# A decoder kernel's first layer: the interleaving tables of two streams, rewritten for four engines

## The chip, the cores and the metric

The kernel runs on one core of a Trainium2 chip. The time is the device time of one execution in microseconds (us). Profiles come from one profiled execution; its span runs from the first instruction's start to the last one's end, and the execution's own time is about 2 us longer than that.

## What is computed

The reference is a decoder of two layers over x of shape (8, 256, 256), eight batches of 256 tokens with 256 features, and a context of (8, 77, 192). Each layer is post-norm: after each block the input is added and a layer norm follows. Cut to what matters:

```python
def layer0(x, ctx):
    # mixer
    xz = x @ W_in.T                       # 256 -> 2 x 512
    xc, z = split(xz)
    xc = silu(causal_conv4(xc) + conv_b)
    B, C, dl = split(xc @ W_xproj.T)      # 16, 16, 512
    dl = softplus(dl)
    bc = sum(B * C, axis=-1)
    y = (dl * xc * bc + D * xc) * silu(z)
    x = layernorm(x + y @ W_out.T)
    # cross attention, 16 heads of 64, 77 context rows
    q, k, v = x @ Wq, ctx @ Wk, ctx @ Wv
    x = layernorm(x + softmax(q @ k.T / 8) @ v @ Wo + bo)
    # 8 experts, the best 2 of each token, and a shared one
    return layernorm(x + moe(x))
def layer1(x, ctx):
    # attention with rotary positions, cross attention, attention with a mask
    ...
```

Everything is float32. The change concerns the order in which the mixer and the cross attention of layer 0 are issued.

## The kernel before, in words

**Tiles and precision.** A batch is held as 2 x 128 tokens of 256 features in `xres` (float32). Matrix products take each operand as a rounded high half and a low half, so a product is three matmuls: high by high, high by low, low by high. ScalarE (ACT) rounds, at L1520; VectorE (DVE) forms the low half of data, at L1908; GpSimd (POOL) forms that of weights, at L2577 and L2633. TensorE (PE) has a few helpers: `mm3` (L169 to L171) issues the three matmuls together; `whole` (L175, L176) issues the two that need only the high half of the data, `rest` (L180) the third once the low half is there; L184, L185 and L189 are the same with the operands swapped; L193 to L197 project the context to keys and values, two batches and up to 308 columns wide. L869 is the transpose, L1064 the scores, L1080 the weighing of values.

**Steps.** Each engine has a generator per batch that issues one step and yields. I name a step by batch and name. In the mixer: xT (transpose of x, rounding, low half), xb (the half of W_in that feeds the convolution), z (the other half, in two steps), B, p0, p1 (the products with W_xproj; before B comes pB), g, sp, dl, yf (DVE's gating), y0, y1 (rounding), y (product with W_out), then add, bs/ba (statistics, L1933 and L1937), ve and rs (the power of the variance, POOL L2589 and L2592) and ln (scaling, DVE L1913). ACT's share of the mixer is also silu (L1560 and L1565), and abs, exp and ln of softplus (L1583, L1590, L1597). DVE's convolution stands at L1913 and L1916. In the cross attention, with X ahead: XxT, Xq0, Xq1 (query projection, two halves), Xs0 to Xs3 (scores of four heads each), Xm, Xu, Xn, Xr on DVE (maximum, subtraction, normalisation), p on POOL (L2616), Xt0 to Xt3 (transposes of the weights), Xo0 to Xo3 (weighing), Xy (product with Wo, one step for each of eight pieces), and POOL's bias add Xbias (L2582). The steps 0.k are the key projection of layer 0. K1.xy are the pieces of layer 1's context projections, made in between and evicted by DVE at L2008.

**Two streams.** Batches 0, 2, 4, 6 are the first stream and 1, 3, 5, 7 the second. Each has its own buffers; the program's names in the order lists below end in 0 and 1 for the two (`ps0`, `r10`, `m10` are the first stream's, `ps1`, `r11`, `m11` the second's). `x0_all(st)` runs `l0` (mixer) and `xattn` over the stream's four batches; the steps of one batch follow those of the batch before it. The streams are merged by `in_turn`:

```python
def in_turn(first, second, after):
    done = 0
    for want in after:
        while done < want:
            next(first, None)
            done += 1
        next(second, None)
```

The list `after` holds one number for each step of the second stream: so many steps of the first stream have been issued on this engine before that step. It is a fixed order, worked out ahead and written into the tables `FIRST` (L42, layer 0), `SECOND` and `LAST` (layer 1), each with a list for PE, ACT, DVE and POOL. `FIRST` is used at L1133 (PE), L1656 (ACT), L2129 (DVE) and L2644 (POOL). SyncE (SP) issues the loads in an order of its own; each waits on semaphores that steps raise. Each engine takes its instructions strictly in the order of the program, and waits between engines are semaphores that a step raises for its batch and name.

**The order before.** The lists of `FIRST` repeat from pair to pair: on PE the same pattern comes back with 59 added, on ACT with 46, on DVE with 63, on POOL with 17. So the pairs 2/3, 4/5 and 6/7 are issued alike, and the pair 0/1 differs where weights still have to come in.

Of the kernel before, what the change touches and what calls it, by code (L numbers as in the profile page):

```python
# [40 lines left out]

FIRST = {  # L42
# [7 lines left out]
    "ACT": [  # L50
# [5 lines left out]
    "DVE": [  # L56
# [7 lines left out]
    "POOL": [  # L64
        1, 4, 5, 8, 9, 11, 13, 13, 13, 13, 13, 13, 15, 16, 16, 16, 16, 18, 21, 22, 25, 26, 28, 30, 30, 30, 30, 30, 30, 32, 33, 33, 33, 33, 35, 38, 39, 42, 43, 45,
        47, 47, 47, 47, 47, 47, 49, 50, 50, 50, 50, 52, 55, 56, 59, 60, 62, 64, 64, 64, 64, 64, 64, 66, 67, 67, 67, 67],
}
SECOND = {
# [2797 lines left out]
```

How the kernel before makes its waits and increments, by code:

```python
        def last_x0(eng):  # L658
            for st in streams:
                eng.wait_ge(*st.x_dve[0].at(st.batches[-1], "ln"))
# [1 line left out]
        def last_moe(eng):  # L662
            eng.wait_ge(*r_pe.at("dn", NT - 1))
            for st in streams:
                eng.wait_ge(*st.n_dve.at(st.batches[0], "ln"))
            eng.wait_ge(*w1s["lo"].at("wp"))
# [1 line left out]
        def last_x1(eng):  # L668
            for st in streams:
                eng.wait_ge(*st.x_pe[1].at(st.batches[-1], "y"))
# [1 line left out]
        def last_q(eng):  # L672
            for st in streams:
                eng.wait_ge(*st.q_dve.at(st.batches[-1], "sim"))
                eng.wait_ge(*st.q_act.at(st.batches[-1], "c2"))
                eng.wait_ge(*st.q_pool.at(st.batches[-1], "bias"))
                eng.wait_ge(d_kp[st.i], 16 * 4)
# [3 lines left out]
        @block.sync  # L681
# [14 lines left out]
            def store0(what, u):  # L696
                slot, done, _ = slot0(what, u)
                sp.wait_ge(*(kv_evk.at(what, u, 3) if what == "k" else kv_ev[0].at(what, u, 1)))
                if what == "k":
                    store_keys(0, u, slot, done)
                else:
                    sp.dma_start(vd[0, P * u:P * (u + 1), :], slot[:, 0:1024]).then_inc(done, 16)
# [1 line left out]
            def store1(u):  # L704
                slot, done, _ = slot1(u)
                sp.wait_ge(*kv_ev[1 if u < 6 else 2].at(u, 3 if u < 4 else 2))
                if u < 4:
                    store_keys(1, u, slot, done)
                else:
# [80 lines left out]
            sp.wait_ge(*gate_dve.at("idx"))
```

## Time and profile before

| | before |
|---|---|
| median of 3 executions (lowest to highest) | 1506.3 us (1503.81 to 1506.79) |
| the profiled execution's own time | 1508.33 us |
| its span | 1506.3 us |
| mean granted TensorE clock, share of full speed | 0.925 |
| PE busy | 1325.1 us (88% of the span) |
| PE weight loads busy | 1098.4 us (73%) |
| DVE busy | 972.1 us (65%) |
| ACT busy | 649.8 us (43%) |
| POOL busy | 424.8 us (28%) |
| chain of work that ended last | PE 69%, DVE 19%, ACT 6% |
| instructions | 27793 |

Busy time is that of one engine's instructions over the whole span; PE's weight loads lie beside its matmuls. The chain of work that ended last is followed back from the last instruction to what released it, so its shares say what the end waited for. Layer 0's mixer and cross attention, which the changed tables order, take about the first 430 us of the span; the rest is layer 0's experts and layer 1. The granted clock has two levels, 1.2 and 2.4 GHz; a share of 0.50 in a stretch is the lower one throughout.

### The profile page before, as it was taken

How to read it: one execution, taken by the hardware profiler on the slowest of the kernel's cores; microseconds unless marked ns; L12 is line 12 of the kernel's file. 1: busy time of each engine (PE TensorE's matmuls, PEld its weight loads, DVE VectorE, ACT ScalarE, POOL GpSimd, SP SyncE). 2: the span in 40 equal slices, each digit the busy share in tenths (PEclk: the TensorE clock that was granted, in tenths of full speed). 3: DMA queues.
4: the chain of work that ended last, by engine and by line, in shares of the span. 5: the costliest groups of instructions: out<-in, count | busy, mean ns of one | idle time of the engine just before them, and what ended most of it. 6: DMA issues, size and time to landing. Idle time of an engine off the chain costs nothing.

```text
span 1506.3 us, 27793 instructions
## 1 busy us (share of the span) xinstructions
PE 1325.1 (88%) x11854; PEld 1098.4 (73%) x11854; DVE 972.1 (65%) x1785; ACT 649.8 (43%) x806; POOL 424.8 (28%) x405
## 2 busy tenths in 40 slices
PE   6899999998989999998789889879978958878886
PEld 6788889888878889997478658748847844646563
DVE  3776767867675446776765946757575645567573
ACT  6554556455542435662244145234334432341513
POOL 5141030310323744675023512703511330000000
PEclk9989999999999999998799899989989965887868
DMA  9371210111060315883001200200200120010000
GB/s 293 134 237 35 48 35 18 32 34 51 1 230 29 109 46 194 276 263 95 11 1 39 67 1 18 81 7 1 77 1 1 43 85 27 18 57 16 2 16 15
DMA packets 46138, 103.33 MB, mean 69 GB/s; under 512 B 4336, under 2 KB 26480, under 8 KB 45120
## 3 DMA queue, kind: packets, MB, share of 16 engines
q1 hardware_dynamic: 42944, 93.18, 18.8%
q0 software_dynamic: 3072, 8.39, 1.7%
q8 instruction: 93, 1.52, 0.4%
q14 instruction: 29, 0.24, 0.0%
HBM read 64.79 MB, written 36.77 MB: 67 GB/s over the span
## 4 chain that ended last, share of the span: by engine, by line
PE 69%; DVE 19%; ACT 6%; POOL 2%; issue 2%; DMA 1%; SPq 0%; POOLq 0%; DVEq 0%; ACTq 0%
DVE sm L1919 9%; PE ps L869 9%; PE ps L169 8%; PE ps L170 8%; PE ps L171 8%; PE ps L1336 4%; PE ps L1064 4%; PE ps L1080 4%; PE ps L184 4%; PE ps L1342 4%; PE ps L189 4%; PE ps L185 3%; ACT m L1778 2%; DVE m L1908 2%; PE ps L175 2%
## 5 line engine op out<-in xcount | busy, mean ns | idle before, releaser
L1520 ACT ACTIVATE m<-ps 128x1024 f32<-128x1024 f32 (+4 forms) x208 | 165.6, 812 | 306.5 <-PE ps L171 107.2
L1919 DVE TENSOR_REDUCE sm<-ps 128x8 f32<-128x2048 f32 (+1 forms) x128 | 193.5, 1533 | 45.3 <-PE ps L1317 25.2
L2589 POOL TENSOR_SCALAR sm<-sm 128x2 f32<-128x2 f32 x40 | 8.8, 219 | 687.0 <-DVE sm L1937 687.0
L1908 DVE TENSOR_TENSOR r<-ps,r 128x512 fp32r<-128x512 f32 (+1 forms) x159 | 116.3, 739 | 122.5 <-ACT r L1520 122.4
L1520 ACT ACTIVATE r<-ps 128x512 fp32r<-128x512 f32 (+1 forms) x159 | 100.9, 639 | 208.1 <-PE ps L869 104.8
L1778 ACT ACTIVATE m<-ps 128x2048 f32<-128x2048 f32 x64 | 119.2, 1876 | 143.2 <-PE ps L1336 143.0
L869 PE MATMUL ps<-cst,m 128*77 128x128 f32 (+2 forms) x1024 | 136.4, 276 | 14.9 <-DVE m L2357 3.6
L869 PEld LDWEIGHTS ps<-cst,m 128*77 128x77 f32 (+2 forms) x1024 | 114.2, 146 | 39.0 <-issue 15.0
L1317 PE MATMUL ps<-m 32*128 32x256 f32 x1024 | 106.3, 553 | 33.3 <-DVE sm L1919 28.7
L1317 PEld LDWEIGHTS ps<-m 32*128 32x128 f32 x1024 | 65.4, 261 | 69.6 <-DVE sm L1919 54.4
L2616 POOL TENSOR_TENSOR m<-m,sm 128x616 f32<-128x616 f32 x64 | 77.0, 1216 | 126.3 <-DVE sm L2092 126.0
L1336 PE MATMUL ps<-m 32*128 32x256 f32 x1024 | 85.8, 465 | 26.1 <-DVE m L2357 22.8
L2357 DVE COPY m<-ps 128x256 f32<-128x256 f32 x64 | 26.9, 422 | 116.9 <-PE ps L1342 116.9
L1336 PEld LDWEIGHTS ps<-m 32*128 32x128 f32 x1024 | 56.2, 221 | 54.8 <-DVE m L2357 42.4
L1342 PE MATMUL ps<-m 128*32 128x256 f32 x1024 | 72.7, 404 | 11.5 <-ACT m L1778 11.1
L1908 DVE TENSOR_TENSOR xres<-ps,xres 128x256 f32<-128x256 f32 (+1 forms) x112 | 51.4, 494 | 48.2 <-PE ps L189 45.5
L169 PE MATMUL ps<-r,w0h 128*128 128x256 f32 x288 | 81.3, 282 | 0.0
L170 PE MATMUL ps<-r,w0h 128*128 128x256 f32 x288 | 81.3, 282 | 0.0
L171 PE MATMUL ps<-r,w0l 128*128 128x256 f32 x288 | 81.1, 282 | 0.0
L169 PE MATMUL ps<-xTall,uw 128*128 128x512 f32 (+1 forms) x216 | 76.1, 352 | 0.2 <-DVE xres L1908 0.2
L170 PE MATMUL ps<-xTall,uw 128*128 128x512 f32 (+1 forms) x216 | 74.9, 347 | 0.0
L171 PE MATMUL ps<-xTall,uw 128*128 128x512 f32 (+1 forms) x216 | 74.7, 346 | 0.0
(322 smaller groups left out, 3606.9 us busy)
## 6 DMA issues: line engine op xcount, KB each, us to landing
raw<-wu_dram SPq DMA_DIRECT2D x20, 768.0 KB, 5.7
keep_dram<-m SPq DMA_DIRECT2D x8, 768.0 KB, 3.7
m<-keep_dram SPq DMA_DIRECT2D x8, 768.0 KB, 4.3
xs_dram<-gsq SPq DMA_DIRECT2D x2, 2944.0 KB, 18.3
ys_dram<-m SPq DMA_DIRECT2D x23, 256.0 KB, 3.1
room<-wu_dram SPq DMA_DIRECT2D x7, 768.0 KB, 4.7
rt<-xs_dram SPq DMA_DIRECT2D x16, 256.0 KB, 3.4
w1raw<-w_dram SPq DMA_DIRECT2D x1, 3840.0 KB, 11.7
```

Source lines behind the costliest of these rows:

```text
L169: pe.matmul(o, l[0], r[0], start=start, stop=False)
L170: pe.matmul(o, l[0], r[1], start=False, stop=False)
L171: return pe.matmul(o, l[1], r[0], start=False, stop=stop)
L869: return pe.transpose(o, i, ident[0:n, 0:n])
L1317: m = pe.matmul(bank(st, a)[:, 256 * j:256 * j + 256], v.qT[r:r + 32, c, 128 * j:128 * j + 128], v.kT[r:r + 32, c, :], start=True, stop=True)
L1336: m = pe.matmul(bank(st, a)[:, 256 * k:256 * k + 256], v.kT[r:r + 32, c, 128 * k:128 * k + 128], v.qT[r:r + 32, c, :], start=True, stop=True)
L1342: m = pe.matmul(bank(st, c)[32 * a:32 * a + 32, 0:256], v.va[:, k, 4 * c + a, :], w[:, a, k, :], start=k == 0, stop=k == 1)
L1520: return act.activation(o, i, ACT.Copy)
L1778: act.activation(v.P, st.ps[:, :], ACT.Exp, scale=0.25).then_inc(sig.up(b, f"e{c}"), 1)
L1908: return dve.tensor_tensor(o, a, b_, op)
L1919: return dve.tensor_reduce(o, i, AX.X, op, **kw)
L2616: pool.tensor_tensor(pw, pw, v.rc[u].unsqueeze(2).to_broadcast([P, 8, CK]), ALU.mult).then_inc(sig.up(b, f"p{u}"), 1)
```

## The change

The four lists of `FIRST` are replaced. No step, instruction, buffer or wait is added or taken away; only where the second stream's steps stand among the first's. The new lists do not repeat from pair to pair: each engine's covers all four batches of a stream. The start of the diff, which says little by itself:

```diff
 FIRST = {
     "PE": [
-        6, 6, 6, 6, 6, 6, 19, 19, 19, 19, 21, 21, 21, 21, 23, 23, 23, 27, 28, 29, 32, 32, 32, 32, 32, 37, 41, 41, 41, 42, 42, 42, 43, 43, 43, 44, 48, 51, 53, 53,
+        5, 6, 6, 6, 6, 6, 21, 21, 21, 21, 21, 21, 21, 21, 23, 23, 23, 27, 27, 27, 27, 27, 27, 27, 38, 38, 40, 40, 40, 40, 41, 41, 41, 41, 43, 47, 47, 49, 53, 53,
...
```

**At the start, on PE.** Behind the key projection of layer 0 (the matmuls of 308 columns) and the transpose of batch 1 (`ps1<-cst,xres`), and ahead of batch 1's product with W_in. One piece of the difference; the twelve added rows are the second half of 0.z, four times these three:

```order
 L197 MATMUL ps1<-ctxB,w0l 128x308
 L869 MATMUL ps1<-cst,xres 128x128 x4
+L169 MATMUL ps0<-r10,w0h 128x256
+L170 MATMUL ps0<-r10,w0h 128x256
+L171 MATMUL ps0<-r10,w0l 128x256
...
 L175 MATMUL ps1<-r11,w0h 128x256
 L176 MATMUL ps1<-r11,w0l 128x256
```

The same twelve are gone from ahead of the key projection, where both halves of 0.z stood before.

**At the first norm, on PE.** From batch 0's product with W_out (0.y) to what follows it. Before:

```order
L184 MATMUL ps0<-w0h,r10 128x256
L185 MATMUL ps0<-w0l,r10 128x256
...
L189 MATMUL ps0<-w0h,r10 128x256 x8
L869 MATMUL ps0<-cst,xres 128x128 x4
L175 MATMUL ps0<-r10,w0h 128x256
L176 MATMUL ps0<-r10,w0l 128x256
```

And of the change:

```order
L189 MATMUL ps0<-w0h,r10 128x256 x8
L184 MATMUL ps1<-w0h,r11 128x256
L185 MATMUL ps1<-w0l,r11 128x256
...
L189 MATMUL ps1<-w0h,r11 128x256 x8
L869 MATMUL ps0<-cst,xres 128x128 x4
```

Batch 1's product with W_out (1.y, 24 matmuls, `ps1`) now stands between 0.y and the transpose 0.XxT; before it stood behind 0.Xq0.

**The same place on DVE.** `m11` and `r11` are batch 1's gating and its low half, the `xres<-ps0,xres` rows batch 0's add, `BN_STATS` and `BN_AGGR` its statistics. Before:

```order
L2000 COPY stage<-ps1 128x512
L1908 TENSOR_TENSOR xres<-ps0,xres 128x256 x2
L1933 BN_STATS sm0<-xres 128x6 x2
L1937 BN_AGGR sm0<-sm0 128x2 x2
L1916 SCALAR_TENSOR_TENSOR m11<-ps1,m11 128x512 x2
L1913 TENSOR_SCALAR xres<-xres,sm0 128x256 x2
L1908 TENSOR_TENSOR m11<-m11,ps1 128x512 x2
L1908 TENSOR_TENSOR r10<-ps0,r10 128x512
L1916 SCALAR_TENSOR_TENSOR m11<-m11,w0f 128x256 x4
L1908 TENSOR_TENSOR r11<-m11,r11 128x512 x2
L1908 TENSOR_TENSOR xres<-ps1,xres 128x256 x2
```

And of the change:

```order
L2000 COPY stage<-ps1 128x512
L1916 SCALAR_TENSOR_TENSOR m11<-ps1,m11 128x512 x2
L1908 TENSOR_TENSOR m11<-m11,ps1 128x512 x2
L1916 SCALAR_TENSOR_TENSOR m11<-m11,w0f 128x256 x2
L1908 TENSOR_TENSOR xres<-ps0,xres 128x256
L1916 SCALAR_TENSOR_TENSOR m11<-m11,w0f 128x256 x2
L1908 TENSOR_TENSOR xres<-ps0,xres 128x256
L1933 BN_STATS sm0<-xres 128x6 x2
L1937 BN_AGGR sm0<-sm0 128x2 x2
L1908 TENSOR_TENSOR r11<-m11,r11 128x512 x2
L1913 TENSOR_SCALAR xres<-xres,sm0 128x256 x2
L1908 TENSOR_TENSOR xres<-ps1,xres 128x256 x2
```

Batch 1's gating and low halves stand ahead of batch 0's scaling now; before, most of them stood behind it.

**In a later pair, on ACT.** Batches 2 and 3, at the rounding of batch 3's transpose (3.xT, `r11<-ps1`). Before:

```order
L1520 ACTIVATE m10<-ps0 128x4x256
L1560 ACT_TABLE_LOAD
L1560 ACTIVATE m10<-ps0 128x1024
L1520 ACTIVATE r11<-ps1 128x512
L1565 ACTIVATE m10<-m10 128x512
L1520 ACTIVATE r10<-m10 128x512
```

And of the change:

```order
L1520 ACTIVATE m10<-ps0 128x4x256
L1520 ACTIVATE r11<-ps1 128x512
L1560 ACT_TABLE_LOAD
L1560 ACTIVATE m10<-ps0 128x1024
L1565 ACTIVATE m10<-m10 128x512
L1520 ACTIVATE r10<-m10 128x512
```

The rounding of 3.xT stands ahead of silu of batch 2's z now; before it stood behind it. On PE, 3.xT stands between the two halves of 2.z; before, behind both.

Further on in each pair, 3.y stands behind 2.Xq1 on PE, 3.g on DVE moves ahead of the first eviction of K1, and in the pairs 4/5 and 6/7 POOL's bias add stands ahead of the powers of the norm. In the attention stretches neighbouring rows of the two streams are swapped on PE, ACT and DVE. The order of SP is the same as before.

## Rows read from the trace of the kernel before

**Rows 1.** Busy us of each engine by stretch (the first line names columns).

```profile
core 0: us, PE busy (x) PEld busy (x) DVE busy (x) ACT busy (x) POOL busy (x), PEclk, DMA share, GB/s
95.00:133.00 38.00, 37.90 (x306) 32.30 (x306) 24.37 (x46) 19.18 (x26) 15.15 (x15) 1.00 0.27 89
133.00:190.00 57.00, 52.12 (x407) 49.17 (x406) 46.57 (x105) 33.04 (x47) 4.55 (x9) 1.00 0.15 32
323.00:380.00 57.00, 51.42 (x411) 48.88 (x410) 46.50 (x103) 33.13 (x47) 4.57 (x9) 1.00 0.11 34
```

**Rows 2.** PE's instructions in order of time, 17 to 95 us: start, duration, instruction, wait before.

```profile
17.33 0.28 PE L169 MATMUL ps<-r,w0h 128*128 128x256 f32 x1
...
18.62 0.28 PE L171 MATMUL ps<-r,w0l 128*128 128x256 f32 x1
19.85 0.38 PE L193 MATMUL ps<-ctxAh,w0h 128*128 128x308 f32 x1 [0.95 <-POOL w0l L2633]
...
32.16 0.30 PE L197 MATMUL ps<-ctxB,w0l 128*128 128x308 f32 x1
...
34.33 0.39 PE L175 MATMUL ps<-r,w0h 128*128 128x256 f32 x1 [0.69 <-ACT r L1520]
...
76.90 1.12 PE L869 MATMUL ps<-cst,xres 128*128 128x128 f32 x4 [6.04 <-DVE xres L1913]
78.77 0.58 PE L175 MATMUL ps<-r,w0h 128*128 128x256 f32 x1 [0.75 <-ACT r L1520]
...
83.66 0.28 PE L184 MATMUL ps<-w0h,r 128*128 128x256 f32 x1
...
94.85 0.39 PE L175 MATMUL ps<-r,w0h 128*128 128x256 f32 x1
```

**Rows 3.** The same view, the pair of batches 2 and 3.

```profile
140.75 0.39 PE L175 MATMUL ps<-r,w0h 128*128 128x256 f32 x1 [1.16 <-ACT r L1520]
...
155.93 0.41 PE L193 MATMUL ps<-ctxAh,kw1h 128*128 128x308 f32 x1 [0.64 <-DVE stage L2008]
...
171.66 0.41 PE L193 MATMUL ps<-ctxAh,kw2h 128*128 128x308 f32 x1 [1.17 <-DVE stage L2008]
...
173.50 0.66 PE L869 MATMUL ps<-cst,xres 128*128 128x128 f32 x4 [0.87 <-DVE xres L1913]
...
174.91 0.39 PE L175 MATMUL ps<-r,w0h 128*128 128x256 f32 x1
...
178.03 0.36 PE L184 MATMUL ps<-w0h,r 128*128 128x256 f32 x1
```

**Rows 4.** ACT, POOL and DVE in order of time, ahead of row 76.90.

```profile
68.59 1.90 ACT L1520 ACTIVATE w0h<-w0raw 128x2048 fp32r<-128x2048 f32 x1
...
70.57 4.51 POOL L2577 TENSOR_TENSOR w0l<-w0raw,w0h 128x2048 fp32r<-128x2048 f32 x1 [29.11 <-ACT w0h L1520]
...
76.11 0.74 DVE L1913 TENSOR_SCALAR xres<-xres,sm 128x256 f32<-128x256 f32 x2 [2.61 <-POOL sm L2592]
```

**Rows 5.** Stretches as in rows 1 (PEclk third from last), and PE's waits.

```profile
70.00:74.00 4.00, 0.87 (x8) 0.66 (x6) 2.99 (x8) 0.49 (x1) 3.43 (x1) 0.87 1.01 342
74.00:82.00 8.00, 4.35 (x19) 3.95 (x20) 5.09 (x11) 1.86 (x3) 2.00 (x3) 0.50 1.03 288
82.00:84.00 2.00, 2.00 (x14) 2.00 (x14) 0.40 (x1) 0.14 (x1) 0.00 (x0) 0.71 1.08 386
430.00:434.00 4.00, 3.73 (x17) 1.47 (x18) 4.00 (x5) 3.25 (x4) 3.01 (x1) 1.00 0.87 265
690.00:692.00 2.00, 0.60 (x3) 0.60 (x3) 1.34 (x3) 0.60 (x1) 0.00 (x0) 0.69 0.00 0
...
430.27 0.40 PE L169 MATMUL ps<-xTall,rwr 128*8 128x512 f32 x1 [1.54 <-DVE xTall L1908]
691.40 0.58 PE L169 MATMUL ps<-xTall,r 128*128 128x256 f32 x1 [3.48 <-DVE r L1908]
```

**Rows 6.** DVE's scaling and POOL's bias add, batches 2 and 1.

```profile
183.62 1.46 POOL L2582 TENSOR_TENSOR xres<-xres,w0f 128x256 f32<-128x256 f32 x2
...
183.68 1.55 DVE L1913 TENSOR_SCALAR xres<-xres,sm 128x256 f32<-128x256 f32 x2 [1.14 <-POOL sm L2592]
```

More of the change, by code:

```diff
@@ L43 @@
     "PE": [
[6 rows of a table removed]
-    "ACT": [
[5 rows of a table removed]
-    "DVE": [
[7 rows of a table removed]
[6 rows of a table added]
+    "ACT": [
[5 rows of a table added]
+    "DVE": [
[7 rows of a table added]
     "POOL": [
-        1, 4, 5, 8, 9, 11, 13, 13, 13, 13, 13, 13, 15, 16, 16, 16, 16, 18, 21, 22, 25, 26, 28, 30, 30, 30, 30, 30, 30, 32, 33, 33, 33, 33, 35, 38, 39, 42, 43, 45,
-        47, 47, 47, 47, 47, 47, 49, 50, 50, 50, 50, 52, 55, 56, 59, 60, 62, 64, 64, 64, 64, 64, 64, 66, 67, 67, 67, 67],
+        3, 3, 3, 12, 12, 12, 12, 12, 12, 12, 12, 12, 15, 15, 15, 20, 20, 20, 20, 20, 26, 26, 26, 26, 29, 29, 29, 29, 29, 32, 32, 32, 41, 41, 41, 41, 41, 46, 46, 46,
+        46, 46, 46, 46, 46, 46, 49, 49, 49, 54, 54, 54, 54, 54, 58, 58, 58, 58, 63, 63, 63, 63, 63, 66, 66, 66],
 }
```

34 rows, old and new, of the table FIRST are left out of this document.

## The prediction, made before the changed kernel was run

> **What bounds the kernel now.** I began with the busy shares by stretch for the first layer, the only part that the change touches [rows 1]. In the stretch that holds a pair's four-head attention (95 to 133 us) TensorE (PE) is busy for 37.90 of 38 us, and later ones look alike: there is nothing to win there, only something to lose. In the stretches that hold a pair's mixer, its projections and the first scores (133 to 190 us, the pair of batches 2 and 3, and 323 to 380 us, that of 6 and 7) it is busy for 52.12 and 51.42 of 57 us, with VectorE (DVE) at about 46.5 beside it. The reader should see that PE's slack in the steady part is about 5 us in each of three pairs, some 15 us in all, and that DVE, at 82% and in strict order, often sets when PE goes on.
>
> Next came PE's rows in order of time, for the waits in brackets. At the start three matter [rows 2]: 0.95 us for the key weights' low half, which GpSimd (POOL) finishes at 19.71; 6.04 us before the transpose of batch 0 for its cross attention; 0.75 us behind that. In the pair of batches 2 and 3 the four longest are 1.16, 0.64, 1.17 and 0.87 us [rows 3]. I call a step by its batch and name, as in the lists of the kernel.
>
> The 6.04 us end in a chain that no order can shorten [rows 4]: ScalarE (ACT) rounds wq at 68.59, POOL forms its low half in 4.51 us, then takes the power for batch 0's norm, DVE scales, and PE may start at 76.90. While PE waits, its clock falls. The mean granted clock is 0.87 from 70 to 74 us, 0.50 from 74 to 82 and 0.71 from 82 to 84 [rows 5], that is, 1.2 GHz from 73.0 to 83.2 us.
>
> **The change, part by part.** Matmuls of 256 columns start 0.118 us apart at 2.4 GHz: the twelve of the second half of 0.z from 17.33 to 18.62 [rows 2]. So the 24 of batch 1's output projection are 24 x 0.118 = 2.8 us. The 24 of 0.Xq0 started at 78.77, and the next step at 83.66 [rows 2], 0.20 us for each, almost all at 1.2 GHz.
>
> *The second half of 0.z moves behind the key projection.* It is 12 matmuls, 1.41 us. Before, they ran between 17.3 and 18.9, while PE would have waited for POOL's low half anyway (row 19.85 is released by it). Now that wait grows from 0.95 to about 2.4 us, and the 12 run after 1.xT, around 33.6. There a wait of 0.69 us for ACT's rounding covers half of them, so PE goes on 0.75 us later. PE stays without a longer wait up to 1.p1, whose result ACT needs before the exponentials, wq and so the chain of [rows 4]: **+0.75 us**. ACT's silu of batch 0 also moves behind wout's rounding, which puts 0.ln1 off by about 1.7 us; DVE takes it some 2 us after it was ready before, so I cost this at nothing. Its cover is thin, and without it the excess over 2 us is added one for one.
>
> *The longer wait may drop the clock.* Bounds come from the trace. After a wait of 1.54 us the clock stayed at 2.4 GHz (1.00 from 430 to 434); in the wait of 6.04 us it fell 2.1 us after the last matmul; in one of 3.48 us it fell after 2.9 us, and was 0.69 over 690 to 692 [rows 5]. The new wait of 2.4 us lies between. If the clock stays, the cost is 0. If it falls at about 21 us, the key projection, which PE did from 19.85 to about 32.5 without a wait [rows 2], runs at roughly 0.55 of their pace; a low stretch of 6.8 us then costs 3.1 us, one of 10.2 us (as that of [rows 5]) 4.6 us. I take 1.2 us, a little under half of the first, since 2.4 us is about midway between the wait that kept the clock and the one that lost it: **+1.2 us**, ends 0 and 4.6. The Trainium skill, page "TensorE: Matmul & The Clock Gate", part 1, says that the array is throttled by default, that sustained activity releases it and idleness takes that back; it speaks against making this wait longer. Read so that the new wait counts as idleness, the term would be 3.1 and the sum -1.35 instead of -3.25 us.
>
> *Batch 1's output projection moves into the 6.04 us.* Before, 0.y was followed by 0.XxT and 0.Xq0, and only then by 1.y. Now 1.y comes first, and DVE takes 1.sp, 1.dl and 1.yf ahead of batch 0's norm. Step by step, without the two terms above: ACT has 1.y0 at about 73.1 and 1.y1 at 74.3, behind wq. DVE has its part of both by 76.4, because batch 0's adds and statistics stand between; POOL's power is ready at about 76.3, and 0.ln ends at 77.1, 0.3 later than before. PE's last eight matmuls of 1.y end at about 77.6. So 0.XxT starts 0.7 us later than 76.90, and the 2.8 us behind it are gone: -2.1. The clock decides the rest: 0.XxT and 0.Xq0 took 1.12 and 4.9 us at 1.2 GHz [rows 2], against 0.66 and 3.1 for batch 2 at the high one [rows 3]. If 1.y's matmuls, spread over the gap, keep the clock up, another 2.3 us go (-4.4); if not, 1.y itself runs slowly and the gain stays at about -2.0. I take the middle, **-3.2 us**, for want of a row nearer to either.
>
> *The order inside each later pair.* The transpose 3.xT now stands between the halves of 2.z, 1.41 us earlier, and ACT rounds it ahead of silu: the wait of 1.16 us [rows 3] goes. What is late next is DVE, which finishes the convolution of batch 2 no sooner. PE then waits about 0.6 us for DVE's 2.xr1, about 0.6 for the first key eviction, now behind the new place of 3.g, and 0.7 each for K1.10 and 2.ln. It reaches the scores 2.Xs0 some 1.7 us earlier. But 3.y now runs after 2.Xq1, so 3.ln falls among the maxima of batch 2. With POOL's bias add beside it that scaling takes 1.55 us [rows 6] instead of the 0.74 of [rows 4], and PE waits about 1 us for 2.Xu0 and 1 us for 3.ln. What is left at 3.Xq0 is about -0.4 us for this pair. For batches 4 and 5 POOL does the bias add ahead of the norm, which takes it out of that collision, so I take -0.9; for 6 and 7, -0.7. Sum **-2.0 us**. Bounds: nothing but the 15 us of waits can be won, and at most a third of them in a chain that DVE paces at 82%, -5; and if the waits at the scores come out 1 us longer in each pair, +1.
>
> *The attention stretches.* All rows that PE, ACT and DVE swap there have PE work to cover them (37.90 of 38 us busy); cost nothing. In the worst place, 0.Xr2 now stands behind 1.Xm0 on DVE, and so POOL's p3 comes some 3 us later, just as PE needs it. Without this cover each us is lost one for one. POOL's and SP's queues carry the same work; SP's order is unchanged, and every load it issues hangs on a semaphore of these steps, so the rest of the program follows the shift.
>
> **Sum.** +0.75 +1.2 -3.2 -2.0 = -3.25 us. The profiled execution took 1508.33 us, its span 1506.3 and 2.0 around it, so it would be 1505.1. It stands 2.0 above the median of the runs shown (1506.3); I carry the difference over: 1506.3 - 3.25 = **1503.0 us**.
>
> **The rivals.**
> - *The gap is filled at the high clock and nothing falls before it.* For: 1.y spreads its 24 matmuls over the gap, and the first wait is barely longer than 2 us. Against: the clock fell 2.1 us into a wait once. Terms: +0.75 +0 -4.4 -2.0 = -5.65: 1500.7.
> - *DVE paces the pairs, and only the start gains.* For: DVE's share of 82%, and that my walk gave back 1.3 of 1.7 us within ten rows. Against: the first wait of each pair plainly goes. Terms: +0.75 +1.2 -3.2 +0 = -1.25: 1505.1.
> - *Slower: the clock falls on the key projection.* One mechanism, at 19 to 32 us on PE: the wait grown to 2.4 us drops the clock for a stretch like that of [rows 5], 4.6 us are lost where PE alone sets the end, and the later gap is filled with slow matmuls. Terms: +0.75 +4.6 -2.0 +0 = +3.35: 1509.7. It decides from the point where more than about 2 us of the first wait are enough to lose the clock and the low stretch lasts over about 6 us. The Trainium skill's page named above would allow it; rows for a wait of just this length are wanting.
>
> **How the numbers follow.** Forecast 0.52, first rival 0.20, second 0.18, third 0.10. A measurement can tell about 0.2%, 3.0 us. The forecast lies right at that bound: its own range is 1501.5 to 1504.5, and I give it 0.30 to faster and 0.22 to the same. Faster 0.30 + 0.20 = 0.50, same 0.22 + 0.18 = 0.40, slower 0.10. The range that should hold 8 in 10 runs from the first rival, with a little more from the pairs (their end of -5 taken half), to just beyond the second: 1499.5 to 1506.5.
>
> **What would show it.** Right: PE's wait before 0.XxT splits into pieces of at most 2.5 us with 1.y between, 1.Xq0 starts 2 to 4.5 us earlier than 94.85, and the wait of 1.16 us before 3.xb is gone. The granted clock from 18 to 32 us says which rival holds: 1.00 throughout speaks for the first, 0.50 over half of it for the third. In the pairs, PE idle in 57 us should go from 4.9 to 4.0 to 4.5 us. Wrong: first keys starting later than 19.85, a wait of over 2 us at 1.pB or 0.Xt0, or PE idle over 1 us in an attention stretch.

## The result and the profile after

The changed kernel took 1493.27 us in the median of five executions (1490.48 to 1496.0), the kernel before 1503.81 (1502.96 to 1506.79) beside it: ratio 0.9919, with a 95% interval of 0.9903 to 0.9935, or 12 us (10 to 15) of 1504. A second series with the unaltered changed kernel gave 0.9927 (0.9902 to 0.9952). I had predicted 1503.0 us, in a range of 1499.5 to 1506.5. It is faster, as forecast, but by 10 to 15 us and not by 3, and lies outside the range.

The page of the changed kernel, its busy times:

```profile
span 1491.3 us, 27793 instructions
PE 1307.7 (88%) x11854; PEld 1088.9 (73%) x11854; DVE 972.4 (65%) x1785; ACT 651.8 (44%) x806; POOL 426.5 (29%) x405
```

The spans of the two profiles differ by 15.0 us. To find where, I took the end of every step from PE's rows in order of time, in both traces. The last step of layer 0's cross attention (7.Xy) ends at 421.07 before and at 411.60 after: 9.5 us. The remaining 5.5 us arise in code that the change does not touch, most of them behind 1360 us; the kernel with only the start changed, below, shows 5.1 of them too. What lies behind 7.Xy took 1085.2 us in the profile of before and 1078.6 to 1085.2 us in the other thirteen profiles of this document. So the 5.5 us are within what one execution differs from the next, with a lower clock beside them (0.77 before against 0.85 after from 1250 to 1400 us), and no part of the explanation. So the question is where 9.5 us come from. By stretch:

| PE's stretch, us | before | changed | gain | predicted |
|---|---|---|---|---|
| start of the keys to end of 1.bc | 45.68 | 46.93 | -1.25 | -1.95 |
| end of 1.bc to end of 1.Xy | 68.01 | 65.84 | +2.17 | +3.2 |
| pair 2/3 (1.Xy to 3.Xy) | 94.64 | 93.01 | +1.63 | +0.4 |
| pair 4/5 | 94.63 | 91.32 | +3.31 | +0.9 |
| pair 6/7 | 98.26 | 94.63 | +3.63 | +0.7 |

The start did about what was said of it in the sum, though not term by term. The pairs gave 8.6 us where I had 2.0. The busy shares, changed kernel (the first row answers to the second of [rows 1], the last to its third; 228 to 285 us was 52.12 of 57 before):

```profile
133.00:190.00 57.00, 53.42 (x417) 50.35 (x417) 47.96 (x109) 33.00 (x47) 6.17 (x10) 1.00 0.15 33
228.00:285.00 57.00, 54.94 (x433) 52.31 (x433) 48.85 (x109) 35.88 (x51) 6.18 (x9) 1.00 0.12 33
323.00:380.00 57.00, 54.69 (x436) 51.77 (x435) 48.95 (x103) 36.39 (x52) 9.51 (x12) 1.00 0.11 34
```

PE's slack, the first number against the second, went from 4.9, 4.9 and 5.6 us to 3.6, 2.1 and 2.3. DVE is busier (48.9 of 57 us), since the same work now fits in less time. PE's rows in order of time with a wait of over 0.25 us, changed kernel, pairs 2/3, 4/5 and 6/7, against [rows 3]:

```profile
145.99 0.44 PE L180 MATMUL ps<-r,w0h 128*48 128x256 f32 x2 [0.28 <-DVE r L1908]
...
163.64 0.36 PE L184 MATMUL ps<-w0h,r 128*128 128x256 f32 x1 [0.87 <-DVE stage L2008]
...
168.90 0.41 PE L193 MATMUL ps<-ctxAh,kw2h 128*128 128x308 f32 x1 [0.64 <-DVE stage L2008]
...
170.12 0.66 PE L869 MATMUL ps<-cst,xres 128*128 128x128 f32 x4 [0.26 <-DVE xres L1913]
...
183.80 1.31 PE L1064 MATMUL ps<-m 128*128 128x154 f32 x8 [0.75 <-DVE m L1908]
...
185.81 0.66 PE L869 MATMUL ps<-cst,xres 128*128 128x128 f32 x4 [0.69 <-DVE xres L1913]
...
260.82 0.41 PE L193 MATMUL ps<-ctxAh,kw2h 128*128 128x308 f32 x1 [0.64 <-DVE stage L2008]
...
262.36 0.41 PE L193 MATMUL ps<-ctxAh,kw2h 128*128 128x308 f32 x1 [0.57 <-DVE stage L2008]
...
264.20 0.41 PE L193 MATMUL ps<-ctxAh,kw2h 128*128 128x308 f32 x1 [0.42 <-DVE m L1916]
...
268.40 0.36 PE L184 MATMUL ps<-w0h,r 128*128 128x256 f32 x1 [0.26 <-issue]
...
353.13 0.39 PE L193 MATMUL ps<-kw2h,ctxAh 128*128 128x256 f32 x1 [0.85 <-DVE stage L2008]
...
355.37 0.39 PE L193 MATMUL ps<-kw2h,ctxAh 128*128 128x256 f32 x1 [0.35 <-DVE stage L2008]
...
368.81 1.31 PE L1064 MATMUL ps<-m 128*128 128x154 f32 x8 [0.88 <-DVE m L1908]
```

The wait of 1.16 us before 3.xb is gone in all three pairs. In 2/3 the two waits at the scores are there that the prediction named (183.80 for 2.Xs2, 185.81 for 3.XxT); in 4/5 neither is.

At the start, PE's rows and two stretches (as in [rows 5]):

```profile
19.87 0.38 PE L193 MATMUL ps<-ctxAh,w0h 128*128 128x308 f32 x1 [3.41 <-POOL w0l L2633]
...
77.33 0.55 PE L184 MATMUL ps<-w0h,r 128*128 128x256 f32 x1 [5.20 <-ACT r L1520]
...
82.26 0.60 PE L869 MATMUL ps<-cst,xres 128*128 128x128 f32 x4
83.60 0.38 PE L175 MATMUL ps<-r,w0h 128*128 128x256 f32 x1 [0.75 <-ACT r L1520]
```

```profile
20.00:22.00 2.00, 2.00 (x10) 2.00 (x11) 2.00 (x6) 1.51 (x2) 0.00 (x0) 0.59 1.04 440
22.00:24.00 2.00, 2.00 (x10) 2.00 (x9) 2.00 (x7) 0.77 (x2) 0.70 (x1) 0.55 0.82 278
```

The wait for the keys' low half is 3.41 us and not 2.4 (x landed 0.7 us earlier in this execution, so PE had finished sooner), and the clock fell behind it, to 0.59 and 0.55 over four microseconds. 1.y does stand in the gap now, but starts only at 77.33, behind a wait of 5.20 us.

### The profile page after: what moved, and what is told of

It reads as the page before. It is cut to its first block, busy times and chain, and to the rows that moved or that the text cites. A ratio compares the mean times of both kernels' runs of the same rounds, so it can differ in the third digit from the quotient of the medians.

```text
span 1491.3 us, 27793 instructions
## 1 busy us (share of the span) xinstructions
PE 1307.7 (88%) x11854; PEld 1088.9 (73%) x11854; DVE 972.4 (65%) x1785; ACT 651.8 (44%) x806; POOL 426.5 (29%) x405
## 3 DMA queue, kind: packets, MB, share of 16 engines
q8 instruction: 93, 1.52, 0.4%
## 4 chain that ended last, share of the span: by engine, by line
PE 32%; DVE 15%; ACT 3%; POOL 2%; issue 1%; DMA 0%; POOLq 0%; DVEq 0%; SPq 0%; ACTq 0%
DVE sm L1919 9%; PE ps L869 6%; PE ps L1336 4%; PE ps L1342 4%; ACT m L1778 2%; PE ps L184 2%; PE ps L1064 2%; PE ps L189 2%; PE ps L1080 2%; PE ps L185 2%; DVE m L1908 2%; PE ps L1455 1%; PE ps L1317 1%; DVE m L2357 1%; PE ps L171 1%
## 5 line engine op out<-in xcount | busy, mean ns | idle before, releaser
L1317 PE MATMUL ps<-m 32*128 32x256 f32 x1024 | 102.5, 536 | 34.7 <-DVE sm L1919 30.2
L1317 PEld LDWEIGHTS ps<-m 32*128 32x128 f32 x1024 | 64.2, 256 | 68.8 <-DVE sm L1919 54.5
L1336 PE MATMUL ps<-m 32*128 32x256 f32 x1024 | 82.6, 449 | 27.5 <-DVE m L2357 23.5
L1336 PEld LDWEIGHTS ps<-m 32*128 32x128 f32 x1024 | 53.5, 210 | 55.7 <-DVE m L2357 43.2
```

What stands on the lines that cost most here:

```text
L1317: m = pe.matmul(bank(st, a)[:, 256 * j:256 * j + 256], v.qT[r:r + 32, c, 128 * j:128 * j + 128], v.kT[r:r + 32, c, :], start=True, stop=True)
L1336: m = pe.matmul(bank(st, a)[:, 256 * k:256 * k + 256], v.kT[r:r + 32, c, 128 * k:128 * k + 128], v.qT[r:r + 32, c, :], start=True, stop=True)
```

## The experiments

Steps' ends, stretches and waits below are read from each run's own trace; they repeat to 0.1 us in the pairs. Edits are given in short form: `new` and `old` are the tables of the changed kernel and of before, and a list is cut where the first step of batch 3 stands (PE 60, ACT 45, DVE 62 or 63, POOL 17 or 18 entries).

### The start alone, and the pairs alone

```diff
-FIRST = new
+FIRST = {e: new[e][:cut[e]] + old[e][cut[e]:] for e in new}
```

> The new order for batches 0 and 1, the order of before for the pairs 2/3, 4/5 and 6/7. My theory, from the two traces laid beside each other: the start gains only about 0.9 us by 133 us, since 1.26 us lost behind the key projection stand against some 2 us won at the first norm. So the time should be 0.5 to 1.5 us below before, ratio 0.999 to 1.000, and the pair 2/3 should show its 4.8 us of PE idle again. Rival: the start sets the stage for the pairs (a different phase between the engines), and more than 3 us of the gain comes with it: ratio below 0.998.

Ratio 0.9997 (0.9984 to 1.0009). 1.Xy ends 2.7 us earlier than before, and the pairs 2/3 and 4/5 last as before, 94.62 and 94.61 us. (6/7 took 99.81, 1.6 more: three waits of 0.91, 0.99 and 0.75 us in a row stand there as before, but in this execution the clock fell behind them, 0.89 from 355 to 370 us.) The rival falls.

```diff
-FIRST = new
+FIRST = {e: old[e][:cut[e]] + new[e][cut[e]:] for e in new}
```

> The order of before for batches 0 and 1, the new order for the three later pairs. My theory: the pairs carry the gain, 1.3 us in the pair 2/3, 3.3 in 4/5 and 3.6 in 6/7, together about 8.2 us by 430 us, where I had predicted 2.0: ratio about 0.994 to 0.995. Rival, that the gain hangs on the start: less than 4 us, ratio above 0.997.

Ratio 0.9947 (0.9935 to 0.9959), 8.0 us (6 to 10). The pairs last 93.01, 91.32 and 94.65 us, to 0.02 us those of the changed kernel. In the traces the two parts are independent, and the pairs carry the gain. The times do not quite add up: 0.5 us (-1.4 to 2.4) and 8.0 us make 8.5, where the whole change gave 12 (10 to 15). The traces have the start alone at 2.7 us, more than its time shows; the rest of the difference stays open.

### The second half of 0.z back

```diff
 "PE": [
-    5, 6, 6, 6, 6, 6, 21, 21, ...
+    6, 6, 6, 6, 6, 6, 21, 21, ...
```

> The changed kernel with one number of PE's list put back, so that both halves of 0.z run ahead of the key projection again; ACT still takes silu of batch 0 behind the rounding of wout. My theory: the 3.41 us of PE idle ahead of the first keys shrink to about 2, the clock stays at 2.4 GHz over 20 to 24 us (1.00 instead of 0.50), and 1.xb starts 0.9 to 1.5 us earlier: 1 to 2 us faster than the changed kernel. Rival: the wait of about 2 us still loses the clock, and then only the 0.45 us of the moved half come back. Second rival: ACT's evictions pace the keys in any case (the wait of 0.78 us before), and nothing is won at 1.xT.

Ratio 0.9916 (0.9904 to 0.9929), no difference that the times can tell from the changed kernel, so the 1 to 2 us that I expected are not in them. The trace tells more. From the start of the keys to that of 1.xT PE took 13.13 us before, 13.60 in the changed kernel's profile, and 12.10 here, 12.05 with the start alone. So with the clock held, the new start is 1.1 us faster than before in this stretch: ACT's silu of batch 0 now stands behind the evictions, and this wait for an eviction, in the trace of before, is gone:

```profile
23.71 0.41 PE L193 MATMUL ps<-ctxAh,w0h 128*128 128x308 f32 x1 [0.78 <-ACT stage L1520]
```

No run moved silu alone, so that it is the cause is read from the rows and not tested. By the end of 1.bc the 1.1 us can no longer be seen: from the start of the keys it is 44.88 to 45.74 us in seven profiles with the changed start and the clock kept, and 45.67, 45.16 and 45.22 in the three with the old start. The fall of the clock costs 1.5 us on top. The half of 0.z costs 0.4 us at the end of 1.xb (16.55 us from the start of the keys here, 16.97 with the start alone), and at 1.bc nothing of it is left: 45.06 against 45.18.

The clock over the keys hangs on the wait ahead of them. PE's row of the first key, and the stretch of 20 to 24 us behind it, for the start alone:

```profile
19.81 0.38 PE L193 MATMUL ps<-ctxAh,w0h 128*128 128x308 f32 x1 [2.44 <-POOL w0l L2633]
```

```profile
20.00:24.00 4.00, 4.00 (x30) 4.00 (x30) 4.00 (x12) 3.01 (x6) 0.76 (x1) 1.00 0.94 362
```

and for the run with POOL's old order, whose start is that of the changed kernel:

```profile
19.20 0.38 PE L193 MATMUL ps<-ctxAh,w0h 128*128 128x308 f32 x1 [2.53 <-POOL w0l L2633]
```

```profile
20.00:24.00 4.00, 4.00 (x20) 4.00 (x19) 4.00 (x11) 1.97 (x5) 1.36 (x1) 0.57 0.90 343
```

2.53 and 3.41 us lost the clock; 2.44, 2.25, 1.82, 1.66, 1.40 and less kept it, in the other runs. Each is one execution, and nothing lies between.

### The norm ahead of the gating

```diff
 "DVE": [
-    2, 2, 7, 9, 9, 9, 9, 9, 10, 13, 14, 21, 21, 21, 21, 21, 21, 21, 22, 26, ...
+    2, 2, 7, 9, 9, 9, 9, 9, 10, 13, 14, 21, 21, 21, 21, 21, 21, 26, 26, 26, ...
```

> The changed kernel with two numbers of DVE's list raised: batch 0's adds, statistics and their aggregation stand ahead of 1.yf0 and 1.yf1. In the changed kernel one instruction of 1.yf0, a scalar_tensor_tensor with both operands in SBUF, took 3.80 us instead of 0.47, and ended at 76.13, just behind POOL's low half of wq (to 75.85). My theory: such an instruction stands still while POOL's runs, and one with an operand in PSUM, or with a single operand, does not. Then here the adds and statistics take their usual 0.41 and 0.43 us beside POOL, 1.yf0 ends at about 76.2 as before, 0.ln ends some 2.5 us earlier, at about 79, and 0.XxT starts 2 to 3 us earlier than 82.25: 2 to 3 us faster than the changed kernel. Rival: the long instruction waited for something else (its operand, a DMA), the adds are held up just as it was, and nothing is won.

What this run was for, first in the changed kernel: DVE in order of time, POOL in order of time, and all DVE instructions of line 1916 with operands in SBUF (shortest, median and longest in ns).

```profile
71.14 1.28 DVE L1908 TENSOR_TENSOR m<-m,ps 128x512 f32<-128x512 f32 x2
72.33 4.20 DVE L1916 SCALAR_TENSOR_TENSOR m<-m,w0f 128x256 f32<-128x256 f32 x2
76.45 0.41 DVE L1908 TENSOR_TENSOR xres<-ps,xres 128x256 f32<-128x256 f32 x1
...
78.02 0.75 DVE L1933 BATCH_NORM_STATS2 sm<-xres 128x6 f32<-128x256 f32 x2
```

```profile
71.34 4.51 POOL L2577 TENSOR_TENSOR w0l<-w0raw,w0h 128x2048 fp32r<-128x2048 f32 x1 [28.92 <-ACT w0h L1520]
```

```profile
L1916 DVE SCALAR_TENSOR_TENSOR m<-m,w0f x128: 466/477/3801, 20.1 to 359.4; 128x256 f32<-128x256 f32 x128
```

And with the norm first, DVE, POOL and PE:

```profile
70.53 0.75 DVE L1908 TENSOR_TENSOR xres<-ps,xres 128x256 f32<-128x256 f32 x2
71.31 0.75 DVE L1933 BATCH_NORM_STATS2 sm<-xres 128x6 f32<-128x256 f32 x2
...
72.20 3.32 DVE L1916 SCALAR_TENSOR_TENSOR m<-m,w0f 128x256 f32<-128x256 f32 x4
```

```profile
69.53 4.51 POOL L2577 TENSOR_TENSOR w0l<-w0raw,w0h 128x2048 fp32r<-128x2048 f32 x1 [28.70 <-ACT w0h L1520]
```

```profile
75.53 0.55 PE L184 MATMUL ps<-w0h,r 128*128 128x256 f32 x1 [5.20 <-ACT r L1520]
...
79.08 1.63 PE L189 MATMUL ps<-w0h,r 128*128 128x256 f32 x8
...
80.55 0.60 PE L869 MATMUL ps<-cst,xres 128*128 128x128 f32 x4
```

The first half of the theory holds. Adds (from PSUM) and statistics (one operand) run at their usual length beside POOL's 4.51 us, while the gating, both of whose tensors are in SBUF, stands still until POOL ends (69.53 + 4.51 = 74.04). The Trainium skill, page "SBUF — State Buffer", section "SBUF: two separate sides", says that DVE and GpSimd share one pair of ports, which an instruction of DVE with two inputs in SBUF, or GpSimd's own, holds for its whole length while the other waits. The rows agree, POOL's start of 71.34 and DVE's end of 76.13 (72.33 + 3.80) among them.

The second half falls. Ratio 0.9912 (0.9899 to 0.9925), the same as the changed kernel's, and from the end of 1.bc to that of 1.Xy PE took 66.00 us against 65.84. The statistics were ready early, but PE still had 1.y ahead of 0.XxT, from 75.53 to 80.55, the clock at 0.50 from 74 to 80 us. What sets this place, by these rows, is the chain wq's low half, gating, rounding, 1.y.

### POOL's low half of wq in eight pieces

```diff
-pool.tensor_tensor(lo[:, a:a + n], raw[:, a:a + n], hi[:, a:a + n], ALU.subtract)
+k = n // 8 if name == "wq" else n
+for a in range(a, a + n, k):
+    pool.tensor_tensor(lo[:, a:a + k], raw[:, a:a + k], hi[:, a:a + k], ALU.subtract)
```

> The changed kernel, where POOL forms the low half of wq in eight instructions of 256 columns instead of one of 2048 (4.51 us). The run with the norm first showed the adds at their usual 0.41 us beside POOL, 1.yf0 standing still until POOL's end, and nothing won, because PE's 1.y, at 1.2 GHz, sets when 0.XxT may start. My theory: DVE's instructions with both operands in SBUF get in between two of POOL's, so none takes over about 1.1 us; 1.yf0 ends some 2 us earlier, and so do 1.y and 0.XxT: 1.5 to 2.5 us faster than the changed kernel, whose clock may even stay up. Rival: POOL keeps its place from one instruction to the next, 1.yf0 still ends with the last of the eight, and nothing is won or 0.5 us lost to the shorter instructions.

DVE, POOL and PE:

```profile
69.90 1.56 DVE L1916 SCALAR_TENSOR_TENSOR m<-m,w0f 128x256 f32<-128x256 f32 x2
```

```profile
68.90 6.81 POOL L2579 TENSOR_TENSOR w0l<-w0raw,w0h 128x256 fp32r<-128x256 f32 x8 [29.15 <-ACT w0h L1520]
```

```profile
72.28 0.36 PE L184 MATMUL ps<-w0h,r 128*128 128x256 f32 x1 [2.57 <-ACT r L1520]
```

Now the two engines take turns: the gating pair takes 1.56 us instead of 4.20, POOL 6.81 for its eight, and PE's wait is 2.57 instead of 5.20. Yet 1.bc to 1.Xy took 66.14 us, no less than 65.84. The clock fell at about 73.2 all the same (0.80 from 72 to 74 us) and stayed at 1.2 GHz to about 83.4 (0.50 from 74 to 80, 0.57 from 80 to 84), with hardly a wait in between; the work starts earlier and runs slowly for longer. Ratio 0.9902 (0.9882 to 0.9922), which the times cannot tell from 0.9919. So in this execution taking the port's share away won nothing.

It can win something, as the last run below shows, which has the eight instructions too. There PE's wait before 1.y is 2.57 us again, and in both 0.XxT starts 13.60 us behind the end of 1.bc, against 14.95 to 15.79 in the nine profiles with one instruction and 1.y ahead of 0.XxT. But there the clock, low from about 72.7 us, was back at about 76.1. The same stretch of this run and of the last one:

```profile
76.00:84.00 8.00, 7.25 (x34) 6.37 (x33) 3.97 (x12) 0.60 (x1) 2.00 (x4) 0.54 1.07 350
```

```profile
76.00:84.00 8.00, 6.60 (x53) 6.13 (x53) 3.70 (x11) 1.62 (x2) 1.72 (x4) 0.99 1.07 360
```

From 1.bc to 1.Xy the last run took 64.04 us, less than any of those nine (65.32 to 66.59). So the port holds 1.y up by 2.6 us and 0.XxT by 1.4 to 2.2, and when the clock comes back decides whether this is still there at the end. Each is one execution, and the times resolve neither.

### One engine's order at a time

```diff
-FIRST = new
+FIRST = {e: old[e] for e in new}
+FIRST["PE"] = old["PE"][:60] + new["PE"][60:]
```

> The kernel before with one list changed: PE takes the new order in the pairs 2/3, 4/5 and 6/7; ACT, DVE and POOL keep theirs. My theory: the order of PE and that of DVE and ACT gain together, because the steps that PE now takes early (3.xT, 2.pB, 2.y, 2.XxT) have to be made ready early by the others. Alone it should give less than 3 of the 8.6 us, and may cost: 3.xT is still rounded behind silu, so the wait before 3.xb stays. Rival: the gain is PE's order alone (work of the other stream put into its waits), and then this kernel comes within 2 us of the one with the new pairs alone, ratio about 0.995.

Ratio 1.0155 (1.0136 to 1.0175), 23 us slower. The pairs last 105.35, 101.25 and 103.81 us. PE's rows, pair 2/3:

```profile
140.97 0.38 PE L175 MATMUL ps<-r,w0h 128*128 128x256 f32 x1 [1.60 <-ACT r L1520]
...
175.84 1.12 PE L869 MATMUL ps<-cst,xres 128*128 128x128 f32 x4 [2.91 <-DVE xres L1913]
...
193.60 2.42 PE L1064 MATMUL ps<-m 128*128 128x154 f32 x8 [3.64 <-DVE m L1908]
```

PE asks for 3.xT, the norm and the scores in the new order while ACT and DVE still make them in the old one. In this pair it is idle for 11.7 us instead of 5.0, and busy for 93.7 us instead of 89.7 with the same instructions: behind the last two of these waits the clock was low (the rows take 1.12 and 2.42 us instead of 0.66 and 1.31). The rival falls far.

```diff
-FIRST["ACT"] = new["ACT"]
+FIRST["ACT"] = new["ACT"][:45] + old["ACT"][45:]
```

> The changed kernel with ACT's old order in the three later pairs. In the prediction, ACT's rounding of 3.xT ahead of silu was what took away the wait of 1.16 us. My theory: that wait comes back in each pair (about 1.1 us before 3.xb, 5.xb, 7.xb), and with it half of it or more at the end of each pair: 2 to 4 us slower than the changed kernel, ratio 0.994 to 0.995 against before. Rival: what follows waits for DVE anyway and the 1.1 us are absorbed, so under 1 us in all.

Ratio 1.0045 (1.003 to 1.0061): the whole gain is gone and more. The pairs last 98.36, 100.06 and 102.60 us, 5.4, 8.7 and 8.0 more than in the changed kernel. The wait at 3.xb came back, longer (1.60 us), but so did others: 1.25 and 1.68 us for DVE's evictions, 1.24 us for ACT's rounding before 3.Xy. I had the direction and a small part of the size. ACT, busy 43% of the time, decides as much as PE's own order.

```diff
-FIRST["POOL"] = new["POOL"]
+FIRST["POOL"] = new["POOL"][:18] + old["POOL"][18:]
```

> The changed kernel with POOL's old order in the three later pairs: the bias adds of 4 and 6 stand behind the powers of 5's and 7's norm again. In the prediction this move was worth 0.5 us for 4/5 and 0.3 for 6/7. My theory now: it is worth little, 0 to 1 us in all, since PE in 4/5 has no wait at 5.XxT. Rival: it is the reason why 4/5 gains 3.3 us and 2/3 only 1.6; then PE's waits at 4.Xs2 and 5.XxT come back (0.7 us each, as at 2.Xs2 and 3.XxT) and the kernel is 2 to 3 us slower than the changed one.

Ratio 0.9914 (0.9896 to 0.9932), as the changed kernel. Only 4/5 is longer, by 0.45 us (91.77), with a wait of 0.37 us at 5.XxT. The rival falls; the size in the prediction, 0.5, was right for 4/5, and the 0.3 for 6/7 is nothing (94.61). The old order of PE alone, or of DVE alone, among the new ones was not tried.

### The order of 4/5 for 2/3 too (three_45)

```diff
+shift = {"PE": 59, "ACT": 46, "DVE": 63, "POOL": 17}
-FIRST[e] = new[e]
+FIRST[e] = new[e][:cut[e]] + [w - shift[e] for w in pair45[e]] + pair45[e] + pair67[e]
```

> The changed kernel, where the pair 2/3 takes the order that the changed kernel has for 4/5, on all four engines. In the changed kernel 2/3 gained 1.6 us and 4/5 3.3. My theory: up to the first scores both gain alike, about 2 us; 2/3 then gives 0.7 back, because PE waits for 2.Xs2 (0.75) and 3.XxT (0.69) while DVE still has 3's norm beside the first maxima, and in 4/5 the whole of 5.XxT and 5.Xq0 stands ahead of 4.Xs2 and covers it. Then 2/3 should gain 3.0 to 3.5 us here, both waits should be gone, and the kernel be 1.4 to 1.9 us faster than the changed one, ratio about 0.991. Rival: the pair 2/3 is another case (batch 1's attention ahead of it ends otherwise, SP's loads are later), the order is out of step with it, and it gains no more than 1.6.

Pair 2/3, PE's waits of over 0.25 us, the whole list:

```profile
166.15 0.41 PE L193 MATMUL ps<-ctxAh,kw2h 128*128 128x308 f32 x1 [0.64 <-DVE stage L2008]
...
167.69 0.41 PE L193 MATMUL ps<-ctxAh,kw2h 128*128 128x308 f32 x1 [0.57 <-DVE stage L2008]
...
169.53 0.41 PE L193 MATMUL ps<-ctxAh,kw2h 128*128 128x308 f32 x1 [0.43 <-DVE m L1916]
...
173.72 0.36 PE L184 MATMUL ps<-w0h,r 128*128 128x256 f32 x1 [0.27 <-issue]
```

The pair lasts 91.29 us, 3.35 less than before and the same as 4/5, and the waits at 2.Xs2 and 3.XxT are gone. The theory holds in the trace to 0.1 us. The time, 0.9924 (0.9903 to 0.9945), does not resolve 1.7 us.

### The old order in the first half of each pair

```diff
-FIRST[e] = new[e]
+FIRST[e] = new[e] with, in each later pair, the old entries up to PE 22, ACT 17, DVE 30
```

> The changed kernel with the old order in the first half of each later pair (PE, ACT and DVE up to the second y and the second ln; POOL and the attention new). My theory: about 1.7 of the 3.3 us of a pair come from the mixer half (3.xT between the halves of 2.z, with ACT's rounding ahead of silu, and y earlier), the rest from the half with the scores. So each pair should show the wait of 1.16 us again and gain 1 to 2 us less than in the changed kernel: 3 to 5 us slower than that. Rival: the halves do not fit together (as with PE's new order alone) and the kernel is slower than before.

Ratio 1.0016 (0.9999 to 1.0033). The wait of 1.16 us is back in each pair. 4/5 lasts 93.08 us, a gain of 1.55 for the half with the scores alone, as the theory says. But 2/3 lasts 98.24 and 6/7 99.13 us, 3.6 and 0.9 longer than before; in 2/3 PE waits 3.65 us at 2.Xs2. DVE's rows say why. Batch 3's add comes first, then batch 2's first maximum; the third row is the add of batch 5:

```profile
181.49 0.90 DVE L1908 TENSOR_TENSOR xres<-ps,xres 128x256 f32<-128x256 f32 x2 [4.32 <-PE ps L189]
...
185.99 0.78 DVE L1919 TENSOR_REDUCE sm<-ps 128x8 f32<-128x616 f32 x1
...
277.01 0.89 DVE L1908 TENSOR_TENSOR xres<-ps,xres 128x256 f32<-128x256 f32 x2 [1.52 <-PE ps L189]
```

In 2/3 this mixed order ends 3.y on PE behind 2.Xq1, while DVE still takes all of batch 3's norm ahead of batch 2's maxima: DVE waits 4.32 us for PE, and then PE 3.65 us for DVE. In 4/5 all of 5.y stands ahead of 4.Xq1, and DVE waits 1.52 us. In 6/7 PE's waits are those of before (5.5 against 5.6 us of those over 0.25), so the half with the scores wins nothing there; the 0.9 us are the clock, 0.72 from 364 to 370 us in this execution. So the split into halves is borne out in one pair only, and in 2/3, where the halves were not made for one another, the rival is right.

### The changed kernel again, and the gains together

> The changed kernel once more, unaltered, to see how far its start differs from one execution to the next. The pairs should repeat to 0.1 us: 1.6, 3.3 and 3.6 us. At the start I expect the clock of the key projection to hang on the wait before it: 3.41 and 2.53 us lost it, 2.44, 1.82, 1.66 and less kept it. Where it is kept, 1.xT ends about 1.1 us before its place in the kernel before, otherwise 0.2 to 0.5 behind that.

The pairs last 92.96, 91.30 and 94.65 us. The wait before the keys was 1.40 us, the clock stayed, keys to 1.xT took 12.08 us, and 1.Xy ended 4.1 us before its place in the kernel before, against 0.9 in the first profile. The same start thus gave 0.9, 1.5, 1.7, 2.0, 2.6, 2.6, 2.7, 3.0 and 4.1 us in nine profiles with it, small edits of it among them. About 1.5 of that spread is the clock over the keys, the rest is when loads land and when the clock comes back behind the gap, between 78 and 83 us. The kernel before has a spread too: its old start ended 0.7 and 0.2 us earlier in two other runs.

```diff
-FIRST = new
+FIRST = three_45 with PE's first entry 6
+wq's low half in eight instructions
```

> Three changes that gained or did not lose, on the changed kernel together: 0.z whole ahead of the keys, POOL's low half of wq in eight instructions, and the order of 4/5 for 2/3 too. My theory: the clock over the keys always holds, 1.7 us from the pair 2/3, up to 1 from the start: ratio 0.989 to 0.990 against before, some 3 us below the changed kernel. Rival: the start gains nothing on the average, and it stands at 0.991.

Ratio 0.9908 (0.9887 to 0.9929), median 1489.37 us (1486.83 to 1494.19). The trace has it 5.4 us ahead of before at 1.Xy, the pairs at 91.26, 91.26 and 94.61 us, and 15.8 us ahead at 7.Xy, where the two profiles of the changed kernel had 9.5 and 12.7. It is the fastest median of all, but its interval covers that of the changed kernel, so that it beats it is shown for layer 0 in the trace and not by the time, which lies nearer to the rival's 0.991 than to 0.989 to 0.990. From 1.bc to 1.Xy it has 64.04 us, with the clock back early, as shown above.

## Why the prediction was wrong

**Where the time is bound: right, but for its ceiling.** PE's slack in the pairs was the place to win, the attention stretches were full and stayed so, and DVE was late next. But I wrote that "at most a third" of the 15 us of waits can be won "in a chain that DVE paces at 82%". The changed kernel won 7.4 of 15.3 in the three stretches, with DVE at 84 to 86%. The share of one busy engine was no ceiling: half the waits were for steps that DVE or ACT could make earlier at another's cost, and the other stream's work covered that cost.

**Second half of 0.z, +0.75: measured +0.4 at 1.xb and nothing at 1.bc.** And beside it I costed ACT's silu behind wout's rounding "at nothing". At 1.xT it goes with -1.1 us, since it had held up the evictions of the keys; I had written that PE did the keys "without a wait", and the wait of 0.78 us at 23.71 was in the trace. At 1.bc nothing of this can be told from the spread either.

**The clock on the keys, +1.2 between 0 and 4.6: measured +1.5 in two of the nine profiles, 0 in the others.** The third rival's mechanism exists, at a third of its price, because the low stretch was 3.5 us and not 10.

**1.y into the 6.04 us, -3.2 between -2.0 and -4.4: measured -2.2** in the changed kernel, -1.4 to -2.7 in the eight other profiles with that order and wq's low half in one instruction, and -1.9 and -4.0 in the two with it in eight. What was wrong here is "DVE has its part of both by 76.4": DVE's gating stood still behind POOL, 1.y0's rounding came at 76.6 instead of 73.1, and DVE's low halves ended at 80.2. The size near the end of -2.0 came true for the reason given there, 1.y ran at 1.2 GHz. With the gating freed 1.y ran mostly at 1.2 GHz too, and the end of -4.4 was all but reached in the one execution in which the clock was back right behind it.

So the start came out near its forecast partly by luck: in this profile a clock term of +1.5 that came in two of nine profiles, and a gain of -2.2 where I had -3.2.

**The order inside each later pair, -2.0: measured -8.6. This is the step that failed**, and it makes up 6.6 us, more than the whole miss in the trace. Four things in it:
- In 2/3 I had PE's new waits at 0.6, 0.6, 0.7, 0.7, 1 and 1 us, 4.6 in all. They are 0.28, 0, 0.64, 0.26, 0.75 and 0.69, 2.6 in all, with one of 0.87 that I had not seen. The places were right but for that one, and the sum 1.1 us too large.
- For 4/5 and 6/7 I did not walk the rows but took 2/3 and added a little for POOL's bias add. The table is not periodic, and that was its point. In 4/5 all of 5.XxT and 5.Xq0 stand ahead of 4.Xs2, and cover DVE's norm beside the first maxima. The whole order of 4/5, moved to 2/3, was worth 1.7 us there, and 1.44 of these are the two waits at the scores; the place of these steps alone was not tried. POOL's share is 0.45 us in one pair. So 3.3 and 3.6 us, where I had 0.9 and 0.7.
- The walk rests on 3.y behind 2.Xq1, which lets 3.ln fall among the maxima. In the new table for PE that is so in 2/3 alone, and what the section on the change says there of each pair holds for this pair: 5.y stands ahead of 4.Xq1, as before, and 7.y in the middle of 6.Xq1.
- Why 6/7 gains 3.6 us is not taken apart. Of batch 7 only 7.XxT stands ahead of 6.Xs2, a wait of 0.88 us is left there, and the half with the scores won nothing by itself.

**Rivals.** "DVE paces the pairs" is refuted. Of "the high clock is kept", the half on the keys is right in most executions. In the gap the clock fell in every profile, and only in the last run did it come back in time to give the rival's price. "Slower" falls: its clock term measured +1.5 and not +4.6, and its 0 for the pairs -8.6.

**The signs.** The wait of 1.16 us went and the attention stretches stayed full, as said. But PE's wait before 1.y stayed in one piece, 5.20 us where I allowed 2.5, 1.Xq0 started 1.6 us earlier and not 2 to 4.5, and PE's idle time in the pairs fell to 3.6, 2.1 and 2.3 us and not to 4.0 to 4.5.

**What the single-engine runs add.** The diff reads as four lists, but it is one schedule. PE's new list with the others' old ones costs 23 us, and ACT's old list among the new ones costs 19. The prediction reckoned with PE and DVE, and named ACT in one place only.

## What to carry to other kernels

Where an order is no longer periodic, walk every period: here the first gained 1.6 us and the others over 3, and copying the order of 4/5 brought its gain to 2/3. Do not cap a gain by the busy share of the second engine while its waits alternate with the first's; count which waits are for work that could be made earlier. And an order over several engines is tested, kept or undone as one piece: an engine at 43% in the wrong order cost more than all that the right one had won.

## What the runs showed of the hardware

An instruction of DVE with both tensors in SBUF, 0.47 us by itself, took 3.80 us beside one of POOL's over 2048 columns, while those that read PSUM or one tensor kept their length; cutting POOL's into eight made the two take turns, 1.56 us for two of DVE's. TensorE's clock fell behind waits of 2.53 and 3.41 us and not behind 2.44, so executions of one kernel differ by 1.5 us at this place; and with PE's wait cut from 5.20 to 2.57 us it fell as well. There it stayed at 1.2 GHz for some 10 us in one execution, most of them filled with work, and for some 3.4 us in another, with the same order and the same wait.
